# The last fifteen tiles of an edge pass: own rows added by GpSimd instead of by a transfer, and the join's softmax behind the sums

## The chip, the cores and the metric

The kernel runs on one core of a Trainium2 chip. The metric is the device time of one execution in microseconds, the median of several runs; lower is better. The engines are called as in the profile: PE (TensorE), DVE (VectorE), ACT (ScalarE), POOL (GpSimd) and SP (SyncE, which here only issues transfers). Each works through its own list of instructions in order; semaphores tie the lists together.

## The reference, cut to what matters

Two graph-attention layers over 20,000 nodes and 10,000 edges sorted by destination, each node also having an edge to itself, and then a small feed-forward block:

```
h = _gatv2(layernorm(x), src, dst, Wl0, bl0, Wr0, br0, att0, bias0)     # layer 0, then elu
h = _gatv2(elu(h),       src, dst, Wl1, bl1, Wr1, br1, att1, bias1)     # layer 1
# _gatv2, for an edge e from src to dst (self edges included):
e      = leaky_relu(xl[src] + xr[dst], 0.2);  logits = einsum('ehc,hc->eh', e, att)
p      = exp(logits - segment_max(logits, dst));  alpha = p / segment_sum(p, dst)
out    = segment_sum(xl[src] * alpha, dst) + bias                        # 4 heads x 128 = 512 columns
x = x + h;  x = x + ffn(layernorm(x))
```

## The kernel before, in words

Both layers end with an *edge pass* (`edge_pass`, called for layer 0 and layer 1). The edges lie in 79 tiles: partition p holds 79 consecutive edges, and tile t is the t-th edge of every partition. The tiles form groups of 9 (eight of them), 4 and 3; a group's softmax shares are ready one step after its last tile.

A tile goes through these steps. POOL gathers rows (`gather`). PE multiplies. DVE adds pairs (`pair_sums`, L807), takes the leaky relu (`leaky`, L813), multiplies one half with the attention vector (`product`, L818) while POOL does the other half (`product_own`, L717), and reduces to logits (`logits`, L824), which needs both halves. `peaks` and `sums_up` run the softmax over a group on DVE, with an `exps` on ACT between them. Then the tile is *weighed*: its source row times its share goes to `w1`, its own row times its share to `w2`, both rings of WR = 6 buffers. ACT does that with eight small instructions (`weigh`, L760 and L762), DVE does it for tiles 71, 73, 75 and 77 (`weigh_too`, L867 and L868). POOL then issues a transfer that adds `w2` onto `w1` for a pair of tiles (`add_own`, L712), and DVE adds `w1` to the running sum (`accumulate`, L878, or four L884 at the first tile of a group), which SP stores to `touched` (L684). A sum frees its `w1` buffer for the tile six later, so `weigh(t)` waits for `accumulate(t-6)`.

All engines walk the same steps k. Lists computed ahead say at which step tile t is weighed (`weigh_at`), its pair's transfer issued (`added_at`) and its sum taken (`sum_at`); within a step the order on each engine is that of the code. The last tiles fall behind the logits, so steps 79 and later hold only weighing, adding and summing.

At the end, partitions that share a destination are *joined*. SP writes the last peak and total of every partition to HBM (`trails`, L689) and reads all of them back into every partition (`others`, L692). DVE computes a softmax over them (L920 to L934, with two exponentials on ACT, four transposes on PE and a copy back on ACT, L777). The sum `first_row` of the partition that owns the destination is fetched by POOL (L729), once DVE has cleared its buffer (the memset L938) and all stores have landed. DVE scales it (L941) and adds the product of PE's four matmuls (L978) to it (L946), and POOL writes it back (L733). POOL's first fetch of the next stage (L993) waits until that has landed: stage `transform_second` after layer 0, the gating stage after layer 1. SP starts the plain loads of that stage (L1033; L1183 and L1184) right after its last store; ACT issues the loads of that stage's constants (L1055 to L1057, 1.5 MB, after layer 0) after its last instruction of the join.

Of the kernel before, what the change touches and what calls it, by code (L numbers as in the profile page):

```python
# [10 lines left out]
ALU = mybir.AluOpType  # L11
# [18 lines left out]
LAST = (4, 3)  # L30
CATCH = 30
TAIL = 9
LEAD = 7
R = 18
OWN, SRC = 0, 1
# [5 lines left out]
WR = 6  # L41
# [532 lines left out]
def edge_signals(nc, c, layer):  # L574

    return group(nc, c, f"e{layer}", "w_loaded w_high w_low b_loaded chain ready transposed featT root z leaky product product_own logit "
              "bottom exps shares weighted weighted_too summed trail_set trail_stored others_loaded "
              "share_exps share_sums share_in share_T share_copied shared joined cleared",
              stored=AR)


def edge_pass(nc, layer, g, s, block):
# [3 lines left out]
    T, w = g["T"], g["w"]  # L586
# [10 lines left out]
    sizes = group_sizes(T)  # L597
    first = [sum(sizes[:i]) for i in range(len(sizes))]
    group_of = [i for i, n in enumerate(sizes) for _ in range(n)]
    NC, W = len(sizes), T + len(sizes)  # L600
# [7 lines left out]
    def columns(buf, i):  # L608
        a, b = span(i)
        return heads(buf[:, a:b])  # L610
# [16 lines left out]
    weigh_at = []  # L627
# [3 lines left out]
        weigh_at.append(max(ready, weigh_at[-1] + (0 if t % 2 and t > T - CATCH else 1)) if t else ready)  # L631
    added_at = [weigh_at[min(t | 1, T - 1)] + 1 for t in range(T)]
    sum_at = [added_at[t] + 1 + t % 2 for t in range(T)]
    steps = sum_at[-1] + 1

    helped = [t for t in range(T - TAIL, T) if t % 2]

# [3 lines left out]
    def due(k, at):  # L641
        return [t for t in range(T) if at[t] == k]

    with ExitStack() as c:
# [6 lines left out]
        w1, w2 = sb("w1", [P, WR, D]), sb("w2", [P, WR, D])  # L651
# [14 lines left out]
        picked = nT[:, :, :, :].rearrange("p b c n -> p (b c n)")[:, 0:2 * H * T].rearrange("p (a h t) -> p a h t", a=2, h=H)  # L666

        got, got0 = g["gathered"], list(g["gathered_before"])
        w_added, w0 = g["w_added"], [layer * 16 * len(range(2 * u, T, WR)) for u in range(WR // 2)]
        for t in range(T):  # L670
            g["gathered_before"][t % R] += 32
        late = [t for t in range(T) if sum_at[t] >= T]
# [23 lines left out]
        @block.gpsimd  # L696
        def _(pool):
            def gather(t):
                u = t % R
                need(pool, s["weighted"], t - R + 1)  # L700
                pool.indirect_dma_start(ring[:, u, 0:2, :].rearrange("p a d -> p (a d)"), None, whole,  # L701
                                        bass.IndirectOffsetOnAxis(g["dst_row"][:, t:t + 1].bitcast(U32), 0)).then_inc(got[u], 16)
                pool.indirect_dma_start(ring[:, u, 2, :], None, halves,
                                        bass.IndirectOffsetOnAxis(g["src_row"][:, t:t + 1].bitcast(U32), 0)).then_inc(got[u], 16)

            def add_own(t):
                if t % 2 == 0 and t < T - 1:
                    return
                b, n = t // 2 * 2 % WR, t % 2 + 1
                pool.wait_ge(s["weighted"], t + 1 - helped_to(t))  # L710
                need(pool, s["weighted_too"], helped_to(t))
                pool.dma_start(w1[:, b:b + n, :], w2[:, b:b + n, :], accum_op=ALU.add).then_inc(w_added[b // 2], 16)  # L712

            def product_own(t):
                b = t % ZR
                pool.wait_ge(s["leaky"], t + 1)
                pool.tensor_tensor(z[:, b, 0, :], z[:, b, 0, :], att[:, :], ALU.mult).then_inc(s["product_own"], 1)  # L717

            for k in range(-LEAD, steps):
                if 0 <= k + 1 < T:  # L720
                    product_own(k + 1)
                for t in due(k, added_at):
                    add_own(t)
                if 0 <= k + LEAD < T:
                    gather(k + LEAD)
            pool.wait_ge(s["cleared"], 1)
            for u in range(AR):
                pool.wait_ge(s["stored"][u], 16 * len(range(u, T, AR)))
            pool.indirect_dma_start(first_row, None, touched[:, :],  # L729
                                    bass.IndirectOffsetOnAxis(g["join_row"][:, 0:1].bitcast(U32), 0),  # L730
                                    bounds_check=P * T - 1, oob_is_err=False).then_inc(g["row_fetched"], 16)
            pool.wait_ge(s["joined"], 1)
            pool.indirect_dma_start(touched[:, :], bass.IndirectOffsetOnAxis(g["join_row"][:, 0:1].bitcast(U32), 0),  # L733
                                    joined, None, bounds_check=P * T - 1, oob_is_err=False).then_inc(g["join_stored"], 16)
            pool.wait_ge(g["join_stored"], 16 * (layer + 1))
# [44 lines left out]
        def _(dve):  # L780
# [64 lines left out]
            def sums_up(t):  # L845
                if not is_last(t):
                    return
                i = group_of[t]
                a, b = span(i)
                q, v = peak[:, 0:b - a], inv[:, 0:b - a]  # L850
                carry = columns2(lg, i)[:, SRC, :, 0]
                dve.wait_ge(s["exps"], i + 1)
                if i:
                    link(dve.tensor_tensor(carry, carry, columns(total, i - 1)[:, :, sizes[i - 1]], ALU.mult))
                link(dve.tensor_tensor(q, lg[:, OWN, a:b], lg[:, SRC, a:b], ALU.add))
                link(dve.tensor_tensor_scan(total[:, a:b], same_w[:, a:b], q, 0.0, ALU.mult, ALU.add))
                link(dve.tensor_tensor_scan(v[:, ::-1], back(gap_w, a + 1, b + 1), back(total, a, b), -BIG, ALU.add, ALU.max))
                link(dve.reciprocal(v, v))
                dve.tensor_tensor(lg[:, :, a:b], lg[:, :, a:b], v.unsqueeze(1).to_broadcast([P, 2, b - a]),
                                  ALU.mult).then_inc(s["shares"], 1)  # L860
# [8 lines left out]

            def accumulate(t):  # L870
                b = t % WR
                dve.wait_ge(w_added[b // 2], w0[b // 2] + 16 * (t // WR + 1))
                need(dve, s["stored"][t % AR], 16 * (t // AR))
                if t == 0:
                    dve.tensor_copy(acc[:, 0, :], w1[:, b, :]).then_inc(s["summed"], 1)
                elif group_of[t] == group_of[t - 1]:
                    dve.wait_ge(s["summed"], t)
                    dve.scalar_tensor_tensor(acc[:, t % AR, :], acc[:, (t - 1) % AR, :], same[:, t:t + 1], w1[:, b, :],  # L878
                                             ALU.mult, ALU.add).then_inc(s["summed"], 1)
                else:  # L880
                    carried = columns2(lg, group_of[t])[:, SRC, :, 0]
                    dve.wait_ge(s["summed"], t)
                    for h in range(H):
                        last = dve.scalar_tensor_tensor(acc[:, t % AR, h * C:(h + 1) * C], acc[:, (t - 1) % AR, h * C:(h + 1) * C],  # L884
                                                        carried[:, h:h + 1], w1[:, b, h * C:(h + 1) * C], ALU.mult, ALU.add)
                    last.then_inc(s["summed"], 1)

            for k in range(-3, T):
                for step, ahead in ((leaky, 2), (logits, 1), (pair_sums, 3), (product, 2), (peaks, 1)):
                    if 0 <= k + ahead < T:  # L890
                        step(k + ahead)
                for t in due(k - 1, weigh_at):
                    if t in helped:
                        weigh_too(t)
                for t in due(k, sum_at):
                    accumulate(t)
                if k >= 0:
                    sums_up(k)
                if k == T - 1:
                    dve.wait_ge(s["shares"], NC)  # L900
                    dve.tensor_copy(trail[:, 0, :], columns(top, NC - 1)[:, :, sizes[-1]]).then_inc(s["trail_set"], 1)
                    dve.tensor_copy(trail[:, 1, :], columns(total, NC - 1)[:, :, sizes[-1]]).then_inc(s["trail_set"], 1)

            for i, n in enumerate(sizes):
                dve.tensor_copy(picked[:, 0, :, first[i]:first[i] + n], columns(top, i)[:, :, 1:])
                last = dve.tensor_copy(picked[:, 1, :, first[i]:first[i] + n], columns(total, i)[:, :, 1:])
# [2 lines left out]
                                   first_end[:, :].unsqueeze(1).to_broadcast([P, 2 * H, T]), ALU.mult))  # L909
            link(dve.tensor_reduce(picked2[:, :, :], picked, AX.X, ALU.add))  # L910
            mine = picked2
            for k in range(T, steps):
                for t in due(k - 1, weigh_at):
                    if t in helped:
                        weigh_too(t)
                for t in due(k, sum_at):
                    if t in late[:-3]:
                        accumulate(t)
            dve.wait_ge(s["others_loaded"], 16)
            link(dve.tensor_tensor(share, others[:, :, 0, :].rearrange("p q h -> p h q"),  # L920
                                   g["joins"][:, :].unsqueeze(1).to_broadcast([P, H, P]), ALU.add))
# [10 lines left out]
            link(dve.tensor_scalar(sums[:, :], sums[:, :], g["no_join"][:, 0:1], None, ALU.add))  # L932
            link(dve.reciprocal(scale4[:, :], sums[:, :]))
            link(dve.tensor_tensor(gain[:, :], gain[:, :], scale4[:, :], ALU.mult))  # L934
            for t in late[-3:]:
                accumulate(t)
            dve.wait_ge(s["summed"], T)
            dve.memset(first_row, 0.0).then_inc(s["cleared"], 1)  # L938
            dve.wait_ge(g["row_fetched"], 16 * (layer + 1))
            for h in range(H):  # L940
                last = dve.tensor_scalar(first_row[:, h * C:(h + 1) * C], first_row[:, h * C:(h + 1) * C], gain[:, h:h + 1], None,  # L941
# [674 lines left out]
```

## Time and profile before

| | us |
|---|---|
| median of three runs (2965.98 to 2967.2) | 2966.5 |
| span of the profiled execution | 2963.6 |
| edge pass of layer 0: from DVE's step 72 to the memset | 60.92 |
| from that memset to POOL's first fetch of the next stage | 20.11 |
| edge pass of layer 1: the same two stretches | 60.23 and 18.03 |

The span runs from the first instruction of the profiled execution to the last; its own time is not listed apart, and the median of the runs is 2.9 us above the span. The four stretches at the ends of the two passes are together 159.3 us, 5.4% of the span, and PE is busy for 32 us of them.

### The profile page before, as it was taken

To read this page: it belongs to the slowest core of one execution; us is meant where nothing else is said; L and a number is where in the kernel's file an instruction comes from. 1 tells how busy PE (TensorE), PEld (TensorE's weight loads), DVE (VectorE), ACT (ScalarE), POOL (GpSimd) and SP (SyncE) were. 2 spreads that over 40 slices of the span, in tenths; PEclk is the share of its full clock that TensorE was granted. 3 is DMA by queue.
4 is the path that set the end of the run, shared out by engine and by line. 5 is a ranking of instruction groups with operands and counts; after the bars stand their busy time and mean duration, and the time that the engine had idled before them with its cause. 6 is when DMAs were issued, how large, how long until landed. Compare 5 with 4: busy or idle time off the path is not lost. (4 is left out here: it accounts for less than half of the span.)

```text
span 2963.6 us, 39697 instructions
## 1 busy us (share of the span) xinstructions
PE 2617.9 (88%) x11179; PEld 1791.7 (60%) x11179; DVE 2496.6 (84%) x5399; ACT 1472.7 (50%) x3557; POOL 1243.8 (42%) x1132
## 2 busy tenths in 40 slices
PE   6999999799897099999988989852999999879997
PEld 5777777443343088888864434321888888746665
DVE  7989998699999567767757999996988888379998
ACT  3545555155555333333321655643777877525554
POOL 0012320578886233333317888843333333014444
PEclk8999999899999599999998999975999999989999
DMA  8999999679897688887856889968999999369999
GB/s 320 341 307 319 320 317 349 204 213 251 246 252 204 196 263 276 271 268 264 264 195 195 240 246 254 249 173 291 369 354 350 346 344 343 118 188 251 249 250 172
DMA packets 320437, 787.01 MB, mean 266 GB/s; under 512 B 53744, under 2 KB 54288, under 8 KB 310010
## 3 DMA queue, kind: packets, MB, share of 16 engines
q1 hardware_dynamic: 220152, 539.68, 51.9%
q0 software_dynamic: 97616, 241.01, 33.5%
q10 hardware_dynamic: 2452, 3.79, 0.4%
q8 instruction: 92, 1.51, 0.2%
q14 instruction: 125, 1.02, 0.1%
HBM read 468.08 MB, written 328.75 MB: 269 GB/s over the span
## 5 line engine op out<-in xcount | busy, mean ns | idle before, releaser
L965 PE MATMUL bank<-wr,nT_e 128*128 128x512 f32 x1264 | 594.2, 614 | 69.5 <-DVE z_e L807 58.6
L1129 PE MATMUL bank<-whi,t_hi 128*128 128x512 f32 x1256 | 524.6, 418 | 23.9 <-DVE t_lo L419 23.9
L1130 PE MATMUL bank<-wlo,t_hi 128*128 128x512 f32 x1256 | 498.9, 397 | 0.0
L1131 PE MATMUL bank<-whi,t_lo 128*128 128x512 f32 x1256 | 497.8, 396 | 0.0
L965 PEld LDWEIGHTS bank<-wr,nT_e 128*128 128x128 f32 x1264 | 234.5, 196 | 327.3 <-issue 288.0
L993 POOL DMA_INDIRECT g_vin<-touched,node_slot x157 | 175.8, 1120 | 313.3 <-DMA g_xin<-in_x 293.3
L993 POOL DMA_INDIRECT vin<-touched,node_slot x157 | 171.5, 1092 | 319.3 <-DMA vin<-rows 305.7
L1129 PEld LDWEIGHTS bank<-whi,t_hi 128*128 128x128 f32 x1256 | 237.9, 189 | 72.5 <-issue 17.1
L701 POOL DMA_INDIRECT ring_e<-rows,dst_row x158 | 209.4, 1325 | 167.8 <-POOLq L85 132.8
L1131 PEld LDWEIGHTS bank<-whi,t_lo 128*128 128x128 f32 x1256 | 238.2, 190 | 57.9
L1130 PEld LDWEIGHTS bank<-wlo,t_hi 128*128 128x128 f32 x1256 | 239.2, 190 | 44.4
L1324 PE MATMUL bank<-g_hi,whi 128*128 128x512 f32 (+1 forms) x640 | 264.8, 414 | 0.0
L1491 POOL DMA_DIRECT2D out<-f_y x157 | 136.0, 866 | 297.1 <-DVE f_y L1527 294.2
L1068 ACT CAST t_hi<-bank 128x512 fp32r<-128x512 f32 (+1 forms) x157 | 92.0, 586 | 328.9 <-PE bank L1131 328.9
L1326 PE MATMUL bank<-g_lo,whi 128*128 128x512 f32 (+1 forms) x640 | 252.6, 395 | 0.0
L1325 PE MATMUL bank<-g_hi,wlo 128*128 128x512 f32 (+1 forms) x640 | 250.9, 392 | 0.0
L717 POOL TENSOR_TENSOR z_e<-z_e,v_att 128x512 f32<-128x512 f32 x158 | 203.3, 1286 | 94.2 <-DVE z_e L813 93.4
L1097 DVE TENSOR_TENSOR t_lo<-bank,t_hi 128x512 fp32r<-128x512 f32 (+1 forms) x157 | 108.2, 689 | 153.6 <-PE bank L1131 153.6
L760 ACT ACTIVATE w_e<-ring_e,lg_e 128x128 f32<-128x128 f32 x600 | 191.2, 391 | 76.6 <-DVE acc_e L878 27.3
L309 POOL DMA_INDIRECT ordered<-pair,place x79 | 77.0, 975 | 356.3 <-DVE place L471 356.3
L745 ACT COPY nT_e<-bank 128x512 f32<-128x512 f32 x158 | 91.7, 580 | 270.4 <-PE bank L957 270.4
L807 DVE TENSOR_TENSOR z_e<-bank,ring_e 128x1024 f32<-128x1024 f32 x158 | 191.8, 1214 | 20.8 <-PE bank L968 14.9
(244 smaller groups left out, 5874.4 us busy)
## 6 DMA issues: line engine op xcount, KB each, us to landing
rows<-t_row SPq DMA_DIRECT2D x312, 512.0 KB, 3.8
touched<-acc_e SPq DMA_DIRECT2D x158, 256.0 KB, 4.6
xin<-in_x SPq DMA_DIRECT2D x156, 256.0 KB, 4.7
xTin<-in_xT SPq DMA_DIRECT2D x156, 256.0 KB, 3.6
w_e<-w_e POOLq DMA_DIRECT2D x78, 512.0 KB, 4.9
vin<-rows SPq DMA_DIRECT2D x156, 256.0 KB, 4.0
g_vin<-rows SPq DMA_DIRECT2D x156, 256.0 KB, 5.8
g_xin<-in_x SPq DMA_DIRECT2D x156, 256.0 KB, 6.3
```

The costliest lines, as they stand in the source:

```text
L701: pool.indirect_dma_start(ring[:, u, 0:2, :].rearrange("p a d -> p (a d)"), None, whole, bass.IndirectOffsetOnAxis(g["dst_row"][:, t:t + 1 ...
L717: pool.tensor_tensor(z[:, b, 0, :], z[:, b, 0, :], att[:, :], ALU.mult).then_inc(s["product_own"], 1)
L760: act.activation(w1[:, b, h * C:(h + 1) * C], ring[:, u, 2, h * C:(h + 1) * C], ACT.Copy, scale=share_of(lg, SRC, t, h))
L807: dve.tensor_tensor(z[:, b, :, :], psR[t % 2][:, :].unsqueeze(1).to_broadcast([P, 2, D]), ring[:, u, 1:3, :], ALU.add).then_inc(s["z"], 1)
L965: pe.matmul(psR[b][:, :], nT[:, b, cc, :], wr[:, cc, :], start=(cc == 0), stop=False)
L993: pool.indirect_dma_start(to, None, g["touched"][layer][:, :], bass.IndirectOffsetOnAxis(g["node_slot"][0:r, t:t + 1].bitcast(U32), 0), bo ...
L1129: pe.matmul(ps, hi[:, cc, :], whi[:, cc, :], start=(cc == 0), stop=False)
L1130: pe.matmul(ps, hi[:, cc, :], wlo[:, cc, :], start=False, stop=False)
L1131: last = pe.matmul(ps, lo[:, cc, :], whi[:, cc, :], start=False, stop=(cc == KC - 1))
L1324: pe.matmul(psG[cc][:, 0:n], whi[:, k, cols], hi[:, b, k, 0:n], start=(k == 0), stop=False)
L1325: pe.matmul(psG[cc][:, 0:n], wlo[:, k, cols], hi[:, b, k, 0:n], start=False, stop=False)
L1326: last = pe.matmul(psG[cc][:, 0:n], whi[:, k, cols], lo[:, b, k, 0:n], start=False, stop=(k == KC - 1))
```

## The change

A constant `NEAR = 15` is added. For the last 15 tiles (64 to 78) there is no adding transfer; POOL adds `w2` to `w1` with an elementwise instruction, one per tile, at the step at which the tile is weighed. The sum of such a tile is taken one step after its weighing, not two to three steps after it. On DVE a helped tile is weighed in its own step, not in the next. At step 78 the last group's shares come before the sums. The gathering of peaks and totals (`picked`) moves behind the sums of steps 79 and 80, and the join's softmax moves behind all sums and behind the memset. SP writes the trails before the store of tile 72 (it was 69).

```
+NEAR = 15
...
+    near = T - NEAR
+    for t in range(near, T):
+        sum_at[t] = max(sum_at[t - 1], weigh_at[t] + 1)
...
             def add_own(t):
-                if t % 2 == 0 and t < T - 1:
+                if t % 2 == 0 or t >= near:
                     return
-                b, n = t // 2 * 2 % WR, t % 2 + 1
+                b = (t - 1) % WR
+                pool.wait_ge(s["weighted"], t + 1)
+                pool.dma_start(w1[:, b:b + 2, :], w2[:, b:b + 2, :], accum_op=ALU.add).then_inc(w_added[b // 2], 16)
+
+            def add_near(t):
+                b = t % WR
                 pool.wait_ge(s["weighted"], t + 1 - helped_to(t))
                 need(pool, s["weighted_too"], helped_to(t))
-                pool.dma_start(w1[:, b:b + n, :], w2[:, b:b + n, :], accum_op=ALU.add).then_inc(w_added[b // 2], 16)
+                pool.tensor_tensor(w1[:, b, :], w1[:, b, :], w2[:, b, :], ALU.add).then_inc(s["near_added"], 1)
...
                 for t in due(k, added_at):
                     add_own(t)
+                for t in due(k, weigh_at):
+                    if t >= near:
+                        add_near(t)
...
             def accumulate(t):
                 b = t % WR
-                dve.wait_ge(w_added[b // 2], w0[b // 2] + 16 * (t // WR + 1))
+                if t < near:
+                    dve.wait_ge(w_added[b // 2], w0[b // 2] + 16 * (t // WR + 1))
+                else:
+                    dve.wait_ge(s["near_added"], t - near + 1)
...
-                for t in due(k - 1, weigh_at):
+                for t in due(k, weigh_at):
+                    if t in helped:
+                        weigh_too(t)
+                if k == T - 1:
+                    sums_up(k)
+                    dve.wait_ge(s["shares"], NC)
...
+                for t in due(k, sum_at):
+                    accumulate(t)
+                if 0 <= k < T - 1:
+                    sums_up(k)
+
+            for k in range(T, steps - 2):
+                for t in due(k, weigh_at):
                     if t in helped:
                         weigh_too(t)
                 for t in due(k, sum_at):
                     accumulate(t)
...
-            for k in range(T, steps):
-                for t in due(k - 1, weigh_at):
-                    if t in helped:
-                        weigh_too(t)
+            for k in range(steps - 2, steps):
                 for t in due(k, sum_at):
-                    if t in late[:-3]:
-                        accumulate(t)
+                    accumulate(t)
+            dve.wait_ge(s["summed"], T)
+            dve.memset(first_row, 0.0).then_inc(s["cleared"], 1)
             dve.wait_ge(s["others_loaded"], 16)
...
-            for t in late[-3:]:
-                accumulate(t)
-            dve.wait_ge(s["summed"], T)
-            dve.memset(first_row, 0.0).then_inc(s["cleared"], 1)
             dve.wait_ge(g["row_fetched"], 16 * (layer + 1))
```

POOL's list at the end of the edge pass of layer 0, before (L717 is `product_own`, L712 the adding transfer):

```order
L717 TENSOR_TENSOR z_e0<-z_e0,v_att0 128x512 [waits e0_leaky] x3
L712 DMA w1_e0<-w2_e0 128x1024 [waits e0_weighted]
L717 TENSOR_TENSOR z_e0<-z_e0,v_att0 128x512 [waits e0_leaky]
L712 DMA w1_e0<-w2_e0 128x1024 [waits e0_weighted]
L717 TENSOR_TENSOR z_e0<-z_e0,v_att0 128x512 [waits e0_leaky]
L712 DMA w1_e0<-w2_e0 128x1024 [waits e0_weighted]
L717 TENSOR_TENSOR z_e0<-z_e0,v_att0 128x512 [waits e0_leaky]
L712 DMA w1_e0<-w2_e0 128x1024 [waits e0_weighted]
L712 DMA w1_e0<-w2_e0 128x1024 [waits e0_weighted_too,e0_weighted] x4
```

And the same place of the changed kernel (L726 is `product_own`, L721 the elementwise add):

```order
L726 TENSOR_TENSOR z_e0<-z_e0,v_att0 128x512 [waits e0_leaky] x3
L715 DMA w1_e0<-w2_e0 128x1024 [waits e0_weighted]
L721 TENSOR_TENSOR w1_e0<-w1_e0,w2_e0 128x512 [waits e0_weighted] x2
L726 TENSOR_TENSOR z_e0<-z_e0,v_att0 128x512 [waits e0_leaky]
L721 TENSOR_TENSOR w1_e0<-w1_e0,w2_e0 128x512 [waits e0_weighted] x2
L726 TENSOR_TENSOR z_e0<-z_e0,v_att0 128x512 [waits e0_leaky]
L721 TENSOR_TENSOR w1_e0<-w1_e0,w2_e0 128x512 [waits e0_weighted] x2
L726 TENSOR_TENSOR z_e0<-z_e0,v_att0 128x512 [waits e0_leaky]
L721 TENSOR_TENSOR w1_e0<-w1_e0,w2_e0 128x512 [waits e0_weighted]
L721 TENSOR_TENSOR w1_e0<-w1_e0,w2_e0 128x512 [waits e0_weighted_too,e0_weighted] x8
```

Each transfer of a pair has become two adds, and the adds of tiles 64 to 69 stand ahead of the last three `product_own`.

DVE's list where the join's softmax begins in the kernel before (L878 and L884 are sums, L920 to L925 the softmax's first half):

```order
L878 SCALAR_TENSOR_TENSOR acc_e0<-acc_e0,same,w1_e0 128x512 x3
L920 TENSOR_TENSOR z_e0<-z_e0,joins 128x512
L922 TENSOR_REDUCE best_e0<-z_e0 128x4
L923 TENSOR_TENSOR best_e0<-best_e0,picked2_e0 128x4
L924 TENSOR_TENSOR gain_e0<-picked2_e0,best_e0 128x4
L925 TENSOR_TENSOR z_e0<-z_e0,best_e0 128x512
```

And in the changed kernel (L893 and L899 are sums, L938 the memset, L940 on the softmax):

```order
L899 SCALAR_TENSOR_TENSOR acc_e0<-acc_e0,lg_e0,w1_e0 128x128 x4
L893 SCALAR_TENSOR_TENSOR acc_e0<-acc_e0,same,w1_e0 128x512 x2
L938 MEMSET w1_e0 128x512
L940 TENSOR_TENSOR z_e0<-z_e0,joins 128x512
L942 TENSOR_REDUCE best_e0<-z_e0 128x4
L943 TENSOR_TENSOR best_e0<-best_e0,picked2_e0 128x4
```

The last three sums and the memset, which stood behind the twelve instructions of the softmax, now stand ahead of them.

## Rows read from the trace of the kernel before

**Rows 1.** The page: the span, and PE's busy tenths in 40 slices of it.

```profile
span 2963.6 us, 39697 instructions
...
PE   6999999799897099999988989852999999879997
```

**Rows 2.** Busy time by stretch: step 72 to memset, memset to first fetch, each layer.

```profile
947.20:1008.12 60.92, 12.02 (x33) 5.03 (x31) 51.62 (x115) 30.84 (x102) 14.17 (x14) 0.63 0.62 151
1008.12:1028.23 20.11, 2.02 (x8) 1.73 (x8) 3.08 (x10) 0.00 (x0) 2.19 (x2) 0.50 0.70 255
1960.85:2021.08 60.23, 12.04 (x33) 5.04 (x31) 51.62 (x116) 30.84 (x102) 14.15 (x14) 0.63 0.60 150
2021.08:2039.11 18.03, 6.16 (x12) 2.71 (x12) 4.16 (x13) 0.00 (x0) 2.17 (x2) 0.50 0.83 295
```

**Rows 3.** Groups by line, DVE, from 947.20 to 1008.12 us.

```profile
L878 DVE SCALAR_TENSOR_TENSOR acc_e<-acc_e,same,w_e 128x512 f32<-128x512 f32 x14 | 10.5, 749 | 2.3 <-DMA w_e<-w_e 1.5
...
L884 DVE SCALAR_TENSOR_TENSOR acc_e<-acc_e,lg_e,w_e 128x128 f32<-128x128 f32 x12 | 3.4, 345 | 4.8 <-DMA w_e<-w_e 4.7
```

**Rows 4.** The same groups, from 1960.85 to 2021.08 us.

```profile
L878 DVE SCALAR_TENSOR_TENSOR acc_e<-acc_e,same,w_e 128x512 f32<-128x512 f32 x14 | 10.5, 749 | 2.5 <-DMA w_e<-w_e 1.7
...
L884 DVE SCALAR_TENSOR_TENSOR acc_e<-acc_e,lg_e,w_e 128x128 f32<-128x128 f32 x12 | 3.4, 344 | 3.9 <-DMA w_e<-w_e 3.8
```

**Rows 5.** Timeline of DVE, layer 0 (start, length, idle before): softmax, sums, memset.

```profile
998.33 1.06 DVE L920 TENSOR_TENSOR z_e<-z_e,joins 128x512 f32<-128x512 f32 x1
...
1005.04 1.14 DVE L884 SCALAR_TENSOR_TENSOR acc_e<-acc_e,lg_e,w_e 128x128 f32<-128x128 f32 x4
...
1008.12 0.48 DVE L938 MEMSET w_e<- 128x512 f32 x1 [0.17 <-DVE acc_e L878]
```

**Rows 6.** Single lines: POOL's and DVE's products, length in ns minimum/median/maximum.

```profile
L717 POOL TENSOR_TENSOR z_e<-z_e,v_att x158: 1258/1281/1331, 561.6 to 1981.2; 128x512 f32<-128x512 f32 x158
L818 DVE TENSOR_TENSOR z_e<-z_e,v_att x158: 673/681/1898, 564.6 to 1982.2; 128x512 f32<-128x512 f32 x158
```

**Rows 7.** Timeline of DVE and of POOL around 879 us, layer 0.

```profile
879.48 1.88 DVE L818 TENSOR_TENSOR z_e<-z_e,v_att 128x512 f32<-128x512 f32 x1
...
879.48 1.31 POOL L717 TENSOR_TENSOR z_e<-z_e,v_att 128x512 f32<-128x512 f32 x1
```

**Rows 8.** Timeline of ACT, layer 0: weighing tile 69, first half.

```profile
970.53 1.28 ACT L760 ACTIVATE w_e<-ring_e,lg_e 128x128 f32<-128x128 f32 x4 [2.86 <-DVE acc_e L884]
```

**Rows 9.** Transfers issued from 955 to 1035 us: KB each, us to landing.

```profile
z_e<-trails SPq DMA_DIRECT2D x1, 512.0 KB, 7.2
...
trails<-trail_e SPq DMA_DIRECT2D x1, 4.0 KB, 3.8
```

**Rows 10.** Transfers issued from 1004 to 1016 us, layer 0.

```profile
wr<-in_Wr ACTq DMA_DIRECT2D x1, 1024.0 KB, 8.4
touched<-acc_e SPq DMA_DIRECT2D x3, 256.0 KB, 7.1
```

**Rows 11.** Transfers issued from 2017 to 2024 us, layer 1.

```profile
touched<-acc_e SPq DMA_DIRECT2D x3, 256.0 KB, 2.0
```

**Rows 12.** Timeline of POOL and DVE from the memset on, both layers.

```profile
1015.69 1.12 POOL L729 DMA_INDIRECT w_e<-touched,join_row  x1 [17.82 <-DMA touched<-acc_e]
...
1024.66 1.06 POOL L733 DMA_INDIRECT touched<-w_e,join_row  x1 [7.85 <-DVE w_e L946]
...
2023.84 1.11 POOL L729 DMA_INDIRECT w_e<-touched,join_row  x1 [13.10 <-DMA touched<-acc_e]
...
2031.51 1.12 DVE L946 SCALAR_TENSOR_TENSOR w_e<-bank,scale_e,w_e 128x128 f32<-128x128 f32 x4
...
2033.46 1.06 POOL L733 DMA_INDIRECT touched<-w_e,join_row  x1 [8.51 <-DVE w_e L946]
```

**Rows 13.** Timeline of ACT and PE in the join, layer 0.

```profile
1004.37 0.59 ACT L777 COPY z_e<-bank 128x512 f32<-128x512 f32 x1 [2.38 <-PE bank L973]
...
1008.10 2.04 PE L978 MATMUL bank<-acc_e,z_e 128*128 128x128 f32 x8 [3.76 <-DVE acc_e L878]
```

More of the change, by code:

```diff
@@ L576, in edge_signals @@
     return group(nc, c, f"e{layer}", "w_loaded w_high w_low b_loaded chain ready transposed featT root z leaky product product_own logit "
-              "bottom exps shares weighted weighted_too summed trail_set trail_stored others_loaded "
+              "bottom exps shares weighted weighted_too near_added summed trail_set trail_stored others_loaded "
               "share_exps share_sums share_in share_T share_copied shared joined cleared",
@@ L668, in edge_pass @@
         got, got0 = g["gathered"], list(g["gathered_before"])
-        w_added, w0 = g["w_added"], [layer * 16 * len(range(2 * u, T, WR)) for u in range(WR // 2)]
+        w_added, w0 = g["w_added"], [layer * 16 * len(range(2 * u, T - NEAR, WR)) for u in range(WR // 2)]
         for t in range(T):
@@ L891, in _ @@
                         step(k + ahead)
-                for t in due(k - 1, weigh_at):
+                for t in due(k, weigh_at):
[4 more added lines that the diff above has]
+                    dve.wait_ge(s["shares"], NC)
+                    dve.tensor_copy(trail[:, 0, :], columns(top, NC - 1)[:, :, sizes[-1]]).then_inc(s["trail_set"], 1)
+                    dve.tensor_copy(trail[:, 1, :], columns(total, NC - 1)[:, :, sizes[-1]]).then_inc(s["trail_set"], 1)
+                for t in due(k, sum_at):
[4 more added lines that the diff above has]
+                for t in due(k, weigh_at):
                     if t in helped:
@@ L896, in _ @@
                     accumulate(t)
[L897 to L902, printed above, removed]
             for i, n in enumerate(sizes):
```

## The prediction

> **What bounds the kernel now.** I read the page first. PE is busy nine tenths of most slices, and there are two holes: the slice from 963 to 1037 us with 0 tenths, and those from 1926 to 2075 us with 5 and 2 [rows 1]. They are the ends of the two edge passes, where the gathers are over and PE waits until the next stage gets its first fetched row. On both sides of a hole the stages run as pipelines of their own, and each begins with POOL's first fetch and SP's loads. So what the change takes from a hole moves all that follows, one to one, and nothing else counts.
>
> The holes have two parts [rows 2]. The first is from DVE's step 72, when the last gather has been issued, to the memset: 60.92 and 60.23 us, of which DVE is busy 51.62 in both. DVE is the bound here. What it waits for, inside its sums, are mostly the adding transfers: 1.5 + 4.7 us in layer 0, 1.7 + 3.8 in layer 1 [rows 3, 4]. The second part, from the memset to the first fetch, takes 20.11 and 18.03 us and is a chain of transfers: last store, row fetch, join, row written back [rows 2, 12].
>
> **The change, part by part.** All sums are made against the span of 2963.6 us [rows 1]; 2.9 us lie between it and the median of the runs, and I keep them.
>
> *The softmax.* In layer 0 it lasts from 998.33 to 1005.04 us, 6.71 us of DVE's time with its wait for ACT, and three sums and the memset stand behind it [rows 5]. Moved behind the memset, it leaves the first part. Layer 1 has the same twelve instructions and the same busy time [rows 2], so 6.71 again. It costs nothing where it goes as long as the row fetch covers it. If it starts 0.45 us after the memset, ACT's copy ends 6.63 us after its start (1004.96 - 998.33) and PE's 2.04 us of matmuls at 8.7 us [rows 5, 13], 9.2 us after the memset. DVE's L946, the first to need them, starts 10.43 us after the memset in layer 1 (2031.51 - 2021.08) [rows 2, 12]. So the cover is 1.2 us.
>
> *The adding transfers.* Their waits go: 6.2 and 5.5 us [rows 3, 4]. Before any new cost, the first parts shrink to 48.0 and 48.0 us.
>
> *The adds on POOL.* No row shows an add, but `product_own` has the same form, 128x512 fp32 with both inputs in SBUF, and takes 1.28 us [rows 6]. Fifteen of them in about 50 us don't fill POOL. They cost DVE time in two ways.
>
> First, waits. I walked the order of the changed kernel from step 72 on, engine by engine, with the lengths of the trace and the waits of the code: a sum 0.75 us and a product 0.68 [rows 3, 6], of which some 0.07 overlaps with the next instruction unless that needs its result, half a weighing as a product, a pass over 1024 columns 1.2, on ACT 2.35 for a weighing (twice the four instructions of [rows 8]), on POOL 1.28. The same walk over the order of before ends 0.9 us short of the trace, so I use differences alone. The one large new wait is at step 77. POOL does the adds of 68 and 69 before `product_own` of tile 78. Tile 69 can't be weighed until the first sum of group 7 (tile 63) frees its buffer, as before [rows 8], so POOL stands for some 4 us in front of a product that is ready, and DVE's last `logits` waits about 2.5 us for it. With 0.6 more in small gaps the walk has 3.1 us of new waits per layer.
>
> Second, the port. The row to look at is L818: 681 ns as a rule, 1898 at most [rows 6]. At 879.48 us it starts together with POOL's product and takes 1.88 us, 0.57 more than POOL's 1.31 [rows 7]: DVE stands until POOL is done and then does its work. Sums, products, weighings and scans on DVE all read two operands from SBUF as L818 does; the reductions and the pair sums out of PSUM don't, and the products of POOL mostly fall beside those. The fifteen adds have no such place. In the walk seven of the fifteen hold up a DVE instruction: a product 0.3 and 0.7, the last step of group 8's shares 1.3, a product 0.1, half of weighing 73 1.1, sum 70 1.2, half of weighing 77 0.9; 5.6 us, of which 0.3 was there before. The others fall beside reductions, or DVE is waiting for that add anyway. So 5.3 us per layer. The bounds are 0 (POOL always gives way, and has the time for it) and 15 x 1.28 = 19.2 us (each add stops DVE for its whole length). I take the walk's figure, since the rule in it is the one of the rows.
>
> The Trainium skill ("SBUF — State Buffer", section "Who interferes with whom") says just this, and it speaks against the change: a VectorE instruction with two SBUF inputs and a GpSimd instruction that reads SBUF exclude each other for a whole instruction, and whoever issues first wins. The trace agrees, with 1.88 us for 0.68. Without the rule the sum below would be 10.6 us better.
>
> So the first part becomes 60.92 - 6.71 - 6.2 + 3.1 + 5.3 = 56.4 us in layer 0, a gain of **4.5 us**, and 60.23 - 6.71 - 5.5 + 8.4 = 56.4 in layer 1, a gain of **3.8 us**.
>
> *From the memset on.* In layer 0 POOL's row fetch starts 7.6 us after the memset, in layer 1 2.8 us after it [rows 2, 12]. The difference is the last stores: they take 7.1 us to land in layer 0, 2.0 in layer 1 [rows 10, 11]. What lies beside them in layer 0 are ACT's loads for the next stage, the 1 MB of `wr` above all, 8.4 us long [rows 10]; ACT issues them right after its copy at 1004.37 us [rows 13], just ahead of the last stores. After the change that copy comes 7 us behind the memset, when the stores have landed. Then layer 0 goes as layer 1 does up to POOL's write of the joined row, 12.4 us after the memset (2033.46 - 2021.08) where it was 16.5 (1024.66 - 1008.12) [rows 2, 12]. From there to the first fetch it took 3.6 us in layer 0, and 5.65 in layer 1, where many loads were under way [rows 2, 12]. Now the moved `wr` is under way there, so between 16.0 and 18.0 us in all, against 20.11. I take 17.0, a gain of **3.1 us**; the bounds are 2.1 and 4.1. In layer 1 nothing of this kind is to be had: 0.
>
> *The rest.* SP's trails and read-back come later; the walk has the read-back issued about 995 us (after store 72 and 3.8 us of trails) and landed at 1002 with its 7.2 us [rows 9], and the softmax starting at 1003. Hidden by 1 us, and by the 1.2 us above. Steps before 72 keep their order on every engine.
>
> Sum: 4.5 + 3.8 + 3.1 = 11.4 us; 2963.6 - 11.4 = 2952.2, and with the 2.9 us around the span **2955 us**.
>
> **The rivals.** *The port costs nothing* (0.2). POOL yields to DVE's stream, or the adds fall into gaps. For it: only a few of the 158 products are held up now, the median being 681 ns [rows 6]. Against it: that is because `product_own` starts when `leaky` ends, beside a reduction. The gain would be 9.8 + 9.1 + 3.1 = 22 us: 2944.5.
>
> *The adds stop DVE for their whole length* (0.04, slower). In the place where the transfers were, DVE's list is one two-operand instruction after the other, and POOL's add starts whenever ACT is done. At 19.2 us per layer the first parts grow by 9.4 and 10.1 us, less the 3.1: 2983. It decides from 0.73 us per add: 30 adds x 0.73 = 22 us, against 12.9 + 12.2 + 3.1 saved less 6.2 of waits. Against it: many adds are waited for by DVE itself, and a wait can't be paid twice.
>
> *The end moves from the sums to the softmax* (0.14): the change doesn't do what it says, because the read-back of the trails lands late. It is issued behind the store of tile 72, and the softmax now begins only after the memset. Each microsecond beyond some 2 is then paid in each layer. If it lands 5 us later than in the walk, 3 us per layer go: 2961, and with the port a little dearer it is no change. Against it: the adding transfers that lay beside it, of 256 KB a tile as the stores are [rows 10], are gone.
>
> **How the numbers follow.** My forecast has 0.62, the free port 0.2, the late softmax 0.14, the slower case 0.04. The forecast's own range is 2948 to 2961: 3 us per layer for the port and the waits, which go together, and 1 us for layer 0's chain. The range for 8 in 10 takes in the free port and half of the late softmax: 2944 to 2962. About 0.2%, 6 us, is what a measurement of this kernel can tell from no change, that is 2960.5. Of the forecast about 0.04 lies above that, of the late softmax half, so faster has 0.84, the same 0.11, slower 0.05.
>
> **What would show it.** In the new profile: DVE's sums without a wait for a transfer, from tile 64 on; the first parts about 56 us long in both layers; two-operand DVE instructions (half weighings, sums) of about 1.3 to 2 us beside POOL's adds, 5 us in all per layer; DVE's last `logits` some 2.5 us behind POOL; the three last stores of layer 0 landing in about 2 us, and POOL's row fetch 3 us after the memset in both layers; no wait for PE of the join's last multiply-add (L946 before). The prediction is wrong if the sums are as late as before with DVE standing at POOL's adds, if the softmax waits for the read-back or L946 for PE, or if the next stage's first products on PE don't come earlier by what the memset did.

## The result and the profile after

The changed kernel takes 2972.23 us (median of 11 runs, 2969.8 to 2974.39), the kernel before 2966.5 beside it (11 runs, 2964.97 to 2967.79). The ratio is 1.0022, with an interval of 1.0015 to 1.003: slower, by about the 0.2% that the prediction took as the least that tells a difference (5.7 us between the medians, against its 6). The forecast was 2955. The profiled execution has a span of 2971.2 us where 2963.6 stood before.

Busy time by stretch, the same four stretches as in [rows 2] (us, then busy time and instructions of PE, PEld, DVE, ACT and POOL, granted clock, DMA share, GB/s):

```profile
947.03:1011.49 64.46, 10.90 (x28) 4.26 (x26) 60.94 (x104) 29.64 (x99) 28.05 (x21) 0.62 0.24 79
1011.49:1029.75 18.26, 3.19 (x12) 2.50 (x12) 8.39 (x22) 1.31 (x3) 2.47 (x3) 0.50 0.85 292
1963.85:2028.30 64.45, 10.89 (x28) 4.26 (x26) 60.93 (x104) 29.64 (x99) 28.05 (x21) 0.63 0.24 79
2028.30:2046.78 18.48, 6.86 (x16) 3.49 (x16) 8.68 (x24) 1.31 (x3) 2.46 (x2) 0.50 0.83 290
```

The first parts are longer, 64.46 and 64.45 us where 60.92 and 60.23 stood and 56.4 was forecast. In them DVE is busy 60.94 us, against 51.62, although it has eleven instructions fewer (104 against 115). So DVE does not wait more, its instructions take longer. Groups of DVE in the first part of layer 0, costliest first (busy us, mean ns, idle before):

```profile
L893 DVE SCALAR_TENSOR_TENSOR acc_e<-acc_e,same,w_e 128x512 f32<-128x512 f32 x14 | 13.0, 926 | 1.3
L836 DVE TENSOR_REDUCE lg_e<-z_e 128x8 f32<-128x1024 f32 x6 | 7.3, 1213 | 1.2 <-POOL z_e L726 1.2
L830 DVE TENSOR_TENSOR z_e<-z_e,v_att 128x512 f32<-128x512 f32 x5 | 6.4, 1276 | 0.0
...
L899 DVE SCALAR_TENSOR_TENSOR acc_e<-acc_e,lg_e,w_e 128x128 f32<-128x128 f32 x12 | 5.4, 516 | 0.0
...
L879 DVE TENSOR_TENSOR w_e<-ring_e,lg_e 128x512 f32<-128x512 f32 x4 | 3.8, 952 | 0.0
```

The waits for transfers are gone, as forecast: no DMA stands behind L893 and L899, where 1.5 and 4.7 us stood in [rows 3]. But a sum takes 926 ns where it took 749, a quarter sum 516 where it took 345, and L830, the product, 1276 where its median is 681 in [rows 6]. The timeline of DVE and then of POOL in the same stretch (start, length, idle before) shows why:

```profile
954.42 3.16 DVE L830 TENSOR_TENSOR z_e<-z_e,v_att 128x512 f32<-128x512 f32 x1
...
967.80 1.22 DVE L866 TENSOR_TENSOR lg_e<-lg_e,total_e 128x4 f32<-128x4 f32 x1
...
981.92 1.22 DVE L836 TENSOR_REDUCE lg_e<-z_e 128x8 f32<-128x1024 f32 x1 [1.22 <-POOL z_e L726]
...
985.49 2.42 DVE L893 SCALAR_TENSOR_TENSOR acc_e<-acc_e,same,w_e 128x512 f32<-128x512 f32 x2
987.83 1.75 DVE L879 TENSOR_TENSOR w_e<-ring_e,lg_e 128x512 f32<-128x512 f32 x1
...
1003.82 1.24 DVE L927 COPY nT_e<-top_e 128x36 f32<-128x36 f32 x1
1004.97 0.17 DVE L928 COPY nT_e<-total_e 128x36 f32<-128x36 f32 x1
```

```profile
954.16 2.87 POOL L721 TENSOR_TENSOR w_e<-w_e 128x512 f32<-128x512 f32 x2
...
967.73 1.26 POOL L721 TENSOR_TENSOR w_e<-w_e 128x512 f32<-128x512 f32 x1 [1.07 <-ACT w_e L774]
...
985.72 3.31 POOL L721 TENSOR_TENSOR w_e<-w_e 128x512 f32<-128x512 f32 x2 [2.67 <-DVE w_e L880]
...
1001.71 3.31 POOL L721 TENSOR_TENSOR w_e<-w_e 128x512 f32<-128x512 f32 x2 [2.65 <-DVE w_e L880]
```

Read the pair at 985 us. POOL's two adds come due while DVE is in the first of two sums. They take 3.31 us instead of 2 x 1.27: each waits, but only for the one DVE instruction that is under way. Then POOL goes, and DVE's next instruction waits: the two sums end 0.79 us late (2.42 against the 1.63 that such a pair takes elsewhere), and the half weighing behind them takes 1.75 us for 0.68. The second sum and the second add by themselves:

```profile
986.37 1.54 DVE L893 SCALAR_TENSOR_TENSOR acc_e<-acc_e,same,w_e 128x512 f32<-128x512 f32 x1
...
987.32 1.71 POOL L721 TENSOR_TENSOR w_e<-w_e 128x512 f32<-128x512 f32 x1
```

The second sum needs the first one's result, so a gap of 0.13 us lies between two sums even where no add is near. The half weighing needs neither sum and starts before the second one has ended (987.83 against 987.91), and still the add goes ahead of it. At 954 us two adds make one product of 0.68 into 3.16; the second of them starts at 955.40, when the product has stood for 1 us, and goes before it too. At 967.80 an instruction of four columns takes 1.22, just behind an add that started at 967.73. In this stretch 14 of the 15 adds hold a DVE instruction, for about 1 us each; one, beside a reduction, does not. Only four of the 14, the pairs at 985 and 1001 us, had to wait for a DVE instruction first.

The second part in layer 0 goes 18.26 us where it took 20.11. POOL's row fetch and write (layer 0, then layer 1), beside [rows 12], and the transfers issued from 1011 to 1030 us (KB each, us to landing), beside [rows 10]:

```profile
1014.21 1.42 POOL L741 DMA_INDIRECT w_e<-touched,join_row  x1 [9.20 <-DMA touched<-acc_e]
1024.00 1.05 POOL L745 DMA_INDIRECT touched<-w_e,join_row  x1 [8.37 <-DVE w_e L962]
1029.75 1.03 POOL L1009 DMA_INDIRECT vin<-touched,node_slot  x1 [4.70 <-DMA touched<-w_e,join_row]
...
2031.03 1.41 POOL L741 DMA_INDIRECT w_e<-touched,join_row  x1 [9.20 <-DMA touched<-acc_e]
```

```profile
wr<-in_Wr ACTq DMA_DIRECT2D x1, 1024.0 KB, 9.9
touched<-acc_e SPq DMA_DIRECT2D x1, 256.0 KB, 2.0
```

The row fetch starts 2.7 us after the memset in both layers, and the last store lands in 2.0 us where three took 7.1: that term came as forecast up to the write of the row, 12.5 us after the memset. From there to the first fetch it takes 5.75 us, 0.1 above the upper bound. DVE begins the softmax (L940) at 1011.89, right after the memset, so it does not wait for the read-back. It scales the fetched row (L957) at 1021.14, and 0.9 us later L962 follows with no wait for PE:

```profile
1022.05 1.13 DVE L962 SCALAR_TENSOR_TENSOR w_e<-bank,scale_e,w_e 128x128 f32<-128x128 f32 x4
```

### The profile page after: what moved, and what is told of

Its sections match the earlier page's. It is cut to its first block and busy times, and to the rows that moved or that the text cites. A ratio compares the mean times of both kernels' runs of the same rounds, so it can differ in the third digit from the quotient of the medians.

```text
span 2971.2 us, 39721 instructions
## 1 busy us (share of the span) xinstructions
PE 2622.2 (88%) x11179; PEld 1793.8 (60%) x11179; DVE 2528.2 (85%) x5399; ACT 1473.4 (50%) x3557; POOL 1272.4 (43%) x1146
## 5 line engine op out<-in xcount | busy, mean ns | idle before, releaser
L981 PE MATMUL bank<-wr,nT_e 128*128 128x512 f32 x1264 | 600.4, 619 | 64.8 <-DVE z_e L819 53.9
L726 POOL TENSOR_TENSOR z_e<-z_e,v_att 128x512 f32<-128x512 f32 x158 | 204.2, 1292 | 86.1 <-DVE z_e L825 85.4
```

Source lines behind the costliest of these rows:

```text
L981: pe.matmul(psR[b][:, :], nT[:, b, cc, :], wr[:, cc, :], start=(cc == 0), stop=False)
```

## The experiments

The softmax's move, the fills, the half adds and the adds on PE with two banks shared their runs of the kernel before, which took 2967.48 us there (22 runs); the copies, the adds on DVE and the last two kernels on PE shared theirs, with 2964.34 us (13 runs). So ratios are compared, and stretches of the profile. A first part is always DVE's step 72 to the memset.

**The softmax's move alone.** The kernel before, with the last three sums and the memset ahead of the softmax and nothing else:

```
             link(dve.tensor_reduce(picked2[:, :, :], picked, AX.X, ALU.add))
             mine = picked2
+            for t in late[-3:]:
+                accumulate(t)
+            dve.wait_ge(s["summed"], T)
+            dve.memset(first_row, 0.0).then_inc(s["cleared"], 1)
             dve.wait_ge(s["others_loaded"], 16)
...
-            for t in late[-3:]:
-                accumulate(t)
-            dve.wait_ge(s["summed"], T)
-            dve.memset(first_row, 0.0).then_inc(s["cleared"], 1)
```

> The kernel before with one part of the change alone: the last three sums and the memset ahead of the join's softmax, the adding transfers kept. Theory (the order is a gain, the adds on POOL a loss): the last two transfers landed at 1000.95 and 1002.98 us in the trace of before, so the last sum ends at about 1003.8 and the memset starts 4.2 us earlier, in layer 1 (landed 2013.86 and 2015.85) 4.3 us; from the memset to the first fetch layer 0 gains 1.85 us and layer 1 loses 0.45, as in the changed kernel: 9.9 us less, 2956.6 us. Rival (what is moved behind the memset comes back in the join, or the next stage doesn't start earlier by what the memset gains): 2966 us.

Measured: 2956.86 us, ratio 0.9963 (0.995 to 0.9976), as the first theory had it. The first parts and the waits for the transfers in layer 0:

```profile
947.68:1004.85 57.17, 10.89 (x28) 4.26 (x26) 46.27 (x103) 29.54 (x99) 14.18 (x14) 0.62 0.63 158
1955.49:2011.63 56.14, 10.90 (x28) 4.26 (x26) 46.27 (x103) 29.53 (x99) 14.14 (x14) 0.64 0.64 161
```

```profile
L878 DVE SCALAR_TENSOR_TENSOR acc_e<-acc_e,same,w_e 128x512 f32<-128x512 f32 x14 | 10.5, 750 | 2.3 <-DMA w_e<-w_e 1.5
...
L884 DVE SCALAR_TENSOR_TENSOR acc_e<-acc_e,lg_e,w_e 128x128 f32<-128x128 f32 x12 | 3.4, 345 | 7.7 <-DMA w_e<-w_e 7.7
```

The first part of layer 0 falls by 3.75 us and not by 6.71, because the softmax had covered 3.0 us of the last adding transfer: the quarter sums now wait 7.7 us for one where they waited 4.7. The rest of the change takes a gain that this half of it alone makes, and turns it into a loss.

**POOL writes without reading.** The changed kernel with a fill of `w2` on POOL in place of each add, so the own rows of the last 15 tiles are left out of the sums; order and waits stay:

```
-                pool.tensor_tensor(w1[:, b, :], w1[:, b, :], w2[:, b, :], ALU.add).then_inc(s["near_added"], 1)
+                pool.memset(w2[:, b, :], 0.0).then_inc(s["near_added"], 1)
```

> The changed kernel; POOL's fifteen adds are memsets of w2 in the same places with the same waits, so they write SBUF and read nothing, and the own rows of the last 15 tiles are left out of the result. Theory of the port (a reading instruction of POOL and a DVE instruction with two operands in SBUF exclude each other): the 15.2 us per layer by which DVE's instructions are longer go, the first parts come to 49 us, 2942 us in all. Rival (the order of POOL's list and the chain over the ring of buffers cost the time): first parts of 62 us or more, 2968 to 2972 us.

Measured: 2946.36 us, ratio 0.9918 (0.9887 to 0.995): 4 us above the port theory's figure, over 21 below the other's, and 2 us from the 2944.5 of the prediction's free port. First parts, and the line itself (instructions, ns minimum/median/maximum):

```profile
948.39:998.95 50.56, 10.90 (x28) 4.25 (x26) 47.04 (x104) 29.54 (x99) 15.28 (x21) 0.64 0.30 101
...
1950.59:2001.14 50.55, 10.91 (x28) 4.26 (x26) 47.03 (x103) 29.53 (x99) 15.29 (x21) 0.65 0.30 101
```

```profile
L721 POOL MEMSET w_e<- x30: 525/525/917, 955.5 to 1993.7; 128x512 f32 x30
```

The first part is 13.90 us shorter than in the changed kernel, DVE's busy time in it also by 13.90 (60.94 - 47.04), and DVE's idle time (3.52 us) is the same in both. So the whole difference is DVE's lengthened instructions; the order, the waits on POOL and the softmax's new place are the same in both and make none of it. The profiled span falls by 25.7 us (to 2945.5) and not by 2 x 13.90, mainly because the stretches before the first hole and behind the second came out 3.1 us longer there. The fills hold up no two-operand instruction. The Trainium skill ("SBUF — State Buffer", section "Who interferes with whom") says that a VectorE instruction with two SBUF inputs contends with a GpSimd instruction that reads SBUF and not with one that only writes it; the two runs agree, with DVE busy for 60.94 us beside adds and 47.04 beside fills.

**Half the length.** The adds over 256 of the 512 columns; the other half of the own rows of these tiles is left out:

```
-                pool.tensor_tensor(w1[:, b, :], w1[:, b, :], w2[:, b, :], ALU.add)...
+                pool.tensor_tensor(w1[:, b, 0:D // 2], w1[:, b, 0:D // 2], w2[:, b, 0:D // 2], ALU.add)...
```

> The changed kernel with POOL's adds over 256 of the 512 columns, the other half of the own rows of the last 15 tiles left out. Theory of the port, held for a whole instruction: an add takes about 0.65 us, holds up DVE about 0.5 us where it was 1.0, and 7 to 8 us per layer go: 2957 us. If what an add costs is a fixed toll for handing the port over: 2970 us. If order and waits are the cause: 2970 us too.

Measured: 2957.88 us, ratio 0.9962 (0.995 to 0.9974), within 1 us of the theory that the loss goes by length. A half add is a little longer than expected (0.77 us, median) and holds DVE less (5.21/15 = 0.35 us in the mean, the 5.21 being 52.25 less the 47.04 beside fills).

```profile
947.77:1003.54 55.77, 10.89 (x28) 4.26 (x26) 52.25 (x103) 29.53 (x99) 20.90 (x21) 0.63 0.27 91
```

**One input instead of two.** A copy from `w1` to `w2` on POOL in place of each add; the own rows of these tiles are left out:

```
-                pool.tensor_tensor(w1[:, b, :], w1[:, b, :], w2[:, b, :], ALU.add).then_inc(s["near_added"], 1)
+                pool.tensor_copy(w2[:, b, :], w1[:, b, :]).then_inc(s["near_added"], 1)
```

> The changed kernel with a copy on POOL (w1 to w2, one input in SBUF) in place of each add; the own rows of the last 15 tiles are left out of the sums. Theory A (it is POOL's reading that excludes DVE's two-operand instructions, so one input is as bad as two): the excess over the run in which POOL only writes (25.8 us for adds of 1.27 us) scales with the copy's length; at 0.6 to 1.0 us per copy 2958 to 2968. Theory B (it takes two inputs on POOL): 2946 to 2948, as with the write alone.

Measured: 2951.24 us, ratio 0.9952 (0.9935 to 0.9969), between the two expectations. The first part decides:

```profile
945.63:999.94 54.31, 10.89 (x28) 4.27 (x26) 50.79 (x103) 29.53 (x99) 19.07 (x21) 0.65 0.28 94
```

```profile
L721 POOL COPY w_e<-w_e x30: 608/672/1187, 952.8 to 1997.3; 128x512 f32<-128x512 f32 x30
```

DVE is busy 50.79 us, 3.75 more than beside the fills, so a POOL instruction with one input holds DVE too; but it holds less than by its length. Set beside the fills, an instruction costs DVE 0.25 us in the mean (copy, 3.75/15, median 0.67 long), 0.35 (half add, 0.77 long) and 0.93 (whole add, 13.90/15, 1.27 long): its median length less 0.34 to 0.42 us each time. Those that hold nothing count in these means: one of fifteen whole adds, three of fifteen half adds or copies. What else is in the difference is not settled.

**The adds on DVE.** The changed kernel, POOL's adds taken out and each add made by DVE right before the tile's sum:

```
...
                 else:
+                    dve.wait_ge(s["weighted"], t + 1 - helped_to(t))
+                    need(dve, s["weighted_too"], helped_to(t))
+                    dve.tensor_tensor(w1[:, b, :], w1[:, b, :], w2[:, b, :], ALU.add).then_inc(s["near_added"], 1)
                     dve.wait_ge(s["near_added"], t - near + 1)
```

> The changed kernel with the 15 adds per layer on DVE itself, right before the sum of each tile. Theory (a POOL add costs DVE some 0.95 us by the port, against 0.62 to 0.7 us that DVE needs for the same add): 2946.4 of the run in which POOL only writes, + 2 x 15 x 0.66 = 20, less 2 of waits = 2964, between 2961 and 2967, so faster than the changed kernel by 5 to 11 us. Rival (the time of the changed kernel lies in its order of the work, not in the port): 2972 or more, since DVE has ten more microseconds of work in each layer.

Measured: 2958.73 us, ratio 0.998 (0.9971 to 0.999). The time is 2 us below my range, but that was added up from the other set of runs; as a share of that set's 2967.48 us the range is 0.9978 to 0.9998, and the ratio lies in it. It is 0.4% less than the changed kernel's ratio. The engine that was to be spared does the work in less time than it loses when POOL does it:

```profile
L880 DVE TENSOR_TENSOR w_e<-w_e 128x512 f32<-128x512 f32 x15 | 10.3, 684 | 0.0
```

```profile
948.63:1005.84 57.21, 10.90 (x28) 4.26 (x26) 55.72 (x118) 29.65 (x99) 7.27 (x6) 0.62 0.27 92
```

The first row is the adds alone, each overlapping a little with the next instruction; the second is the first part. DVE is busy 55.72 us in it, 9.55 more than in the kernel with six banks on PE below (46.17), where neither DVE nor POOL adds: 0.64 each, against 0.93 lost to an add on POOL.

**The adds on PE, two banks.** In place of POOL's adds, two multiplications by the identity add `w1` and `w2` up in PSUM, and DVE's sum reads the bank:

```
+                added = w1[:, b, :] if t < near else psN[t % 2][:, :]
...
+            for t in range(near, T):
+                b = t % WR
+                pe.wait_ge(s["weighted"], t + 1 - helped_to(t))
+                need(pe, s["weighted_too"], helped_to(t))
+                if t >= near + 2:
+                    pe.wait_ge(s["summed"], t - 1)
+                pe.matmul(psN[t % 2][:, :], ident[:, :], w1[:, b, :], start=True, stop=False)
+                pe.matmul(psN[t % 2][:, :], ident[:, :], w2[:, b, :], start=False, stop=True).then_inc(s["near_added"], 1)
```

> The changed kernel with the adds of the last 15 tiles on PE: two matmuls of 128x512 with the identity add w1 and w2 up in a bank of PSUM, and the sum reads it there. Theory of the port: no POOL instruction beside DVE's sums and none of DVE's sums with two operands in SBUF, so the 15.2 us and the 1.2 us of waiting behind POOL go, and PE's two matmuls (about 1.9 us at the low clock) are hidden but for a few: first parts of 49 to 51 us, 2944 us. Rival 1 (order and waits): 2965 us or more. Rival 2 (PE at half its clock takes POOL's place as the one that is waited for): first parts of 56 us, 2955 us.

Measured: 2956.55 us, ratio 0.9958 (0.9946 to 0.9971), nearest to the second rival. DVE's instructions have their old lengths, but it waits for PE, and the first part is 56.45 us long (945.75 to 1002.20; DVE's sums in it, then PE's timeline, then two stretches with the granted clock, the third number from the right):

```profile
L885 DVE SCALAR_TENSOR_TENSOR acc_e<-acc_e,same,bank 128x512 f32<-128x512 f32 x13 | 9.7, 746 | 9.1 <-PE bank L986 8.5
```

```profile
960.14 1.02 PE L986 MATMUL bank<-w_e,ident 128*128 128x512 f32 x2
970.01 2.04 PE L985 MATMUL bank<-w_e,ident 128*128 128x512 f32 x2 [8.86 <-DVE acc_e L885]
```

```profile
957.40:961.00 3.60, 3.60 (x9) 1.44 (x8) 3.46 (x9) 2.02 (x8) 0.84 (x1) 1.00 0.01 2
969.50:973.50 4.00, 3.49 (x4) 1.51 (x5) 1.11 (x2) 4.00 (x15) 0.00 (x0) 0.50 0.51 197
```

After the adds of the first two tiles PE stands 8.86 us until a sum frees a bank, and the next pair of passes then takes 2.04 us instead of 1.02: the granted clock is 1.00 (2.4 GHz) from 957.4 to 961.0 us and 0.50 (1.2 GHz) from 969.5 to 973.5, behind the idle stretch. Both multiplications of that tile take 3.76 us (970.01 to 973.77), where the expectation had about 1.9. The rival named the clock; the timeline says that the want of a bank comes first.

**The adds on PE, six banks.** The same with the four banks that the edge pass has done with:

```
-    ..., psN = ..., banks[6:8]
+    ..., psN = ..., banks[6:8] + banks[2:4] + banks[0:2]
...
-                if t >= near + 2:
-                    pe.wait_ge(s["summed"], t - 1)
+                if t == near + 2:
+                    pe.wait_ge(s["z"], T)
+                if t >= near + 6:
+                    pe.wait_ge(s["summed"], t - 5)
```

> The changed kernel with the adds of the last 15 tiles made by PE (two multiplications by the identity into one PSUM bank), the sums reading that bank, and six banks in turn (two of its own and the four that the edge pass has done with) in place of the two of the run before, where DVE stood 8 to 9 us per layer for PE. Theory (with the port out of the way the first part is DVE's own work and nothing else): the waits for PE go, the stretch from the last gather to the memset falls from 64.0 us to 55 to 57 in each layer, below the 58.1 of the run in which POOL only writes; the time is 2956.5 - 15 = about 2941, between 2937 and 2945. Rival (PE stands idle and then runs at half clock, so that the adds stay late whatever the number of banks): 2950 to 2956.

Measured: 2939.93 us, ratio 0.9912 (0.9896 to 0.9929): the lowest of all, level with the variant below, and it computes the whole reference.

```profile
946.57:995.03 48.46, 39.31 (x88) 15.91 (x86) 46.17 (x104) 29.54 (x99) 7.28 (x6) 0.96 0.31 105
```

The first part is 48.46 us. Without transfers, POOL and new waits the prediction had it at 48.0. Counted from the last gather, as the expectation counts (939.04 to 995.03 us), it is 55.99, within the 55 to 57. Against the changed kernel the two first parts are 32.0 us shorter and the profiled span is 32.5 us shorter (2938.7), so nearly all of the gain lies in them.

A last variant, which lets a buffer be weighed anew as soon as PE has read it, by ACT as here and in the same way by DVE:

```
-                need(act, s["summed"], t - WR + 1)
+                need(act, s["near_added"], t - WR - near + 1) if t - WR >= near else need(act, s["summed"], t - WR + 1)
...
```

> As the run with six banks, and the weighing of tile t waits for PE's add of tile t-6 and no longer for DVE's sum of it, since the sum reads PSUM. Theory (DVE's list is the bound, ACT has time): within 2 us of the run with six banks, 2939 to 2943. Rival (ACT's weighing, late because it waits for the sums, is what DVE waits for): 3 to 6 us less than that run.

Measured: 2940.01 us, ratio 0.9915 (0.9899 to 0.9932), no different. ACT is not what bounds the stretch.

## Why the prediction was wrong

*The softmax*: right. It left the first part and did not come back as a wait: in the changed kernel DVE goes from the memset through the softmax without standing for the read-back, and L962 follows L957 with no wait for PE. The rival of the late softmax did not happen, and not only because the sums were late: with six banks on PE the memset is at 995.03 us and the softmax goes on at 995.43 without a wait. The 6.71 and the 6.2 us could be added only because both edits were made; alone, the move gives 3.75 in layer 0.

*The adding transfers*: right, 6.2 and 5.5 us of waits are gone, and 48.0 us for what is left is borne out by 48.46 on PE.

*Waits for POOL*: 3.1 us forecast. The fills give 50.56 - 48.0 = 2.6, of which the wait at step 77 is 1.23 us where the walk had 2.5, and 0.87 us (47.04 - 46.17) are mostly a product of POOL that moved to a place where it holds a DVE instruction, which the prediction had at nothing.

***The port*: the step that failed.** The term was 5.3 us per layer and is 13.90. The rule, that the two engines exclude each other, was right; what failed is the walk's count of the adds that hold DVE. It had seven of the fifteen, 5.6 us or 0.8 each, and set the others beside reductions or behind a wait of DVE that was there anyway. On the chip 14 of 15 hold DVE, at 13.90/14 = 0.99 us, or 0.93 in the mean over all fifteen; one alone falls beside a reduction. The doubled count makes most of the difference. The walk's turns are not on record one by one, so which of them let the eight go free stays open; the runs show that an add goes as soon as the DVE instruction under way ends, though DVE's next one is due, and that it holds instructions of a few columns and a copy as well. The row that I used, 879.48 us, shows both starting together and says nothing of the case of a stream, which is the case here. So this came out as the slower rival, which I gave 0.04. Its threshold was 0.73 us per add, and the measured 0.93 lies above it; its price, 19.2 us per layer, was too high.

*From the memset on*: 3.1 us forecast in layer 0, 1.85 measured (20.11 to 18.26), 0.25 below the bound. In layer 1 0.45 us were lost where 0 was forecast. The `wr` load, issued at 1018.70 us and 9.9 us long, lies beside the row's way back from 1024.00 on and is the likely reason in layer 0, but this is not shown: twelve loads of 256 KB by SP (`vin`) lie there as well, and no run takes either away.

The sum, from the forecast span of 2952.2: first parts 2 x 8.06 = +16.1 (8.6 of port less 0.5 of waits in each), second parts 1.26 + 0.45 = +1.7, and +1.3 that lie between the holes (step 72 of layer 1 comes 3.00 us late, the first fetch before it 1.52, and step 72 of layer 0 0.17 early). That is 2971.3, against 2971.2. Why the stage between takes 1.5 us more is not settled.

## What to carry to other kernels

Work that is moved from a queue to POOL is not free because POOL has time: if it reads SBUF beside a dense stream of two-operand instructions on DVE, count each of its instructions against DVE (here an add of 1.27 us at 0.93, shorter ones at less than half of their length), and compare that with the time DVE would need to do the work itself (here 0.64 us). PE and a few PSUM banks that lie idle can do the same add with no port in the way, if there are enough banks for PE to run ahead of the reader. And when two edits are made at once, time them apart: one of them here was a gain of 0.4% and hid in the other's loss.

## What the runs showed that was not expected

Where an add meets DVE's dense stream, the stream does not win: the four adds that had to wait went when the DVE instruction under way ended, with the next one due (985 and 1001 us). They do not simply take turns either, since at 954 us a second add passed the product that stood waiting; what decides is open. How small the DVE instruction is makes no difference: one of 128x4 took 1.22 us. And a copy with a single input, `nT_e<-top_e` of 128x36, took 1.24 us for 0.17 beside an add, so DVE's side does not need a second input; the prediction counted only instructions with two. The Trainium skill ("SBUF — State Buffer", section "Who interferes with whom") says that copies can contend as well, under conditions on their operands; the row agrees, with 1.24 us. Two copies of 128x4 took 0.30 and 0.23 us beside a fill, where they take 0.17 and 0.16, so beside copies even a POOL instruction that only writes is not quite free.
